# A routed expert layer: nine full expert tiles behind half of the dispatch, thirty behind all of it, and shared tiles among them

## The reference

```python
h = _layernorm(x, axis=-1) * (1 + ca) + sa
x = x + ga * _L0_attn_ref(h, ...)     # 1024 training steps of a small MLP, then q through it
h = _layernorm(x, axis=-1) * (1 + cb) + sb
x = x + gb * _L0_ffn_ref(h, ...)
```

```python
logits = jnp.einsum('btd,ed->bte', x, w_router)
probs = jax.nn.softmax(logits, axis=-1)
vals, idx = jax.lax.top_k(probs, TOP_K)                  # TOP_K = 2
hs = jax.nn.gelu(jnp.einsum('btd,fd->btf', x, Ws1) + bs1)
acc = jnp.einsum('btf,df->btd', hs, Ws2) + bs2
h = jax.nn.gelu(jnp.einsum('btd,efd->btef', x, W1) + b1)
y = jnp.einsum('btef,edf->bted', h, W2) + b2
return SCALE * (acc + jnp.einsum('bted,bte->btd', y, gates))
```

## Time and profile before

| | us |
|---|---|
| median of 3 runs | 688.48 (681.39 to 690.98) |
| profiled execution | 682.79 |
| its span, first to last instruction | 680.9 |
| PE, DVE, POOL, ACT busy | 594.7, 428.7, 350.4, 315.2 |
| 39 expert tiles, first to last product | 148.6 |

### The profile page before, as it was taken

How to read it: one execution, slowest core, us unless ns; L and a number is a source line. 1 busy time by engine, 2 the same in 40 slices (tenths; PEclk the granted TensorE clock), 3 DMA queues, 4 the chain that set the end, 5 groups by cost and what they waited for, 6 DMA issues and landing times. The chain is left out here.

```text
span 680.9 us, 14547 instructions
## 1 busy us (share of the span) xinstructions
PE 594.7 (87%) x4322; PEld 519.4 (76%) x4322; DVE 428.7 (63%) x1766; ACT 315.2 (46%) x996; POOL 350.4 (51%) x556
## 2 busy tenths in 40 slices
PE   1459999999999999999965898899399999999927
PEld 1339999999999999999843776677289989999912
DVE  2846888888888888888847767374044545445406
ACT  1455666666666666666513342353044444434300
POOL 1025666666666666666526386575615455454520
PEclk9999999999999999999978787889799999999969
DMA  9059900000000000000000011111737678787457
GB/s 213 6 230 414 410 32 1 1 0 0 0 0 0 0 0 0 0 0 1 2 0 1 4 49 37 40 45 38 221 88 215 217 212 239 210 230 227 145 183 210
DMA packets 42739, 66.76 MB, mean 98 GB/s; under 512 B 7394, under 2 KB 30692, under 8 KB 42692
## 3 DMA queue, kind: packets, MB, share of 16 engines
q1 hardware_dynamic: 31908, 52.74, 25.0%
q0 software_dynamic: 4544, 9.45, 3.8%
q10 hardware_dynamic: 6240, 4.00, 2.2%
HBM read 36.25 MB, written 29.92 MB: 97 GB/s over the span
## 5 line engine op out<-in xcount | busy, mean ns | idle before, releaser
L1770 POOL DMA_INDIRECT ys<-yo,dst x78 | 74.6, 957 | 87.7 <-DVE yo L1685 71.8
L1473 ACT ACTIVATE hid<-bank,slab 128x256 f32<-128x256 f32 x156 | 63.5, 474 | 87.9 <-PE bank L1364 79.5
L1762 POOL DMA_INDIRECT xs<-hrow,slot_i x64 | 68.9, 1077 | 35.1 <-issue 23.8
L1375 PEld LDWEIGHTS bank<-slab,hid 128*128 128x128 f32 x624 | 75.6, 192 | 2.0
L1364 PE MATMUL bank<-hg,slab 128*128 128x256 f32 x312 | 74.7, 382 | 1.7 <-issue 0.7
L1375 PE MATMUL bank<-slab,hid 128*128 128x128 f32 x624 | 75.8, 275 | 0.0
L1364 PEld LDWEIGHTS bank<-hg,slab 128*128 128x128 f32 x312 | 56.2, 190 | 9.5 <-issue 2.5
L1465 ACT ACTIVATE hs<-bank,sb 128x256 f32<-128x256 f32 x64 | 26.2, 474 | 62.7 <-PE bank L1330 42.0
L1346 PE MATMUL bank<-sw,hs 128*128 128x128 f32 x256 | 37.7, 304 | 9.9 <-ACT hs L1465 7.4
L1346 PEld LDWEIGHTS bank<-sw,hs 128*128 128x128 f32 x256 | 34.1, 212 | 16.1 <-ACT hs L1465 10.5
L1668 DVE SCALAR_TENSOR_TENSOR row<-xt,etab 128x2 f32<-128x2 f32 x39 | 8.6, 220 | 58.1 <-DMA ys<-yo,dst 48.5
(11 more groups left out here) (313 smaller groups left out, 1813.7 us busy)
## 6 DMA issues: line engine op xcount, KB each, us to landing
slab<-in_slabs_dram SPq DMA_DIRECT2D x39, 578.0 KB
xs<-fill SPq DMA_DIRECT2D x34, 528.0 KB
xt<-xs SPq DMA_DIRECT2D x39, 132.0 KB
xr<-in_L_attn_x_dram SPq DMA_DIRECT2D x8, 256.0 KB, 8.9
yg<-ys SPq DMA_DIRECT2D x4, 512.0 KB, 8.8
yg<-ys ACTq DMA_DIRECT2D x4, 512.0 KB, 9.7
ys<-yo,dst POOLq DMA_INDIRECT x78
xs<-hrow,slot_i POOLq DMA_INDIRECT x64
```

What stands on the lines that cost most here:

```text
L1375: mm = pe.matmul(bank[4 + j % 2][:, s * D:(s + 1) * D], hid[j % 2][:, n, s * P:(s + 1) * P], slab[j % RW][:, F + n * P:F + (n + 1) * P], s ...
L1473: nc.scalar.activation(hid[j % 2][:, n, :], e_half(j, n), ACT.Gelu_apprx_tanh, bias=slab[j % RW][:, 2 * F + n:2 * F + n + 1]).then_inc(e_x, 1)
L1762: pool.indirect_dma_start(out=xs[:, :], out_offset=bass.IndirectOffsetOnAxis(ap=slot_i[:, i, c:c + 1], axis=0), in_=hrow[:, c, :], in_offs ...
L1770: pool.indirect_dma_start(out=ys[:, :], out_offset=bass.IndirectOffsetOnAxis(ap=dst[r][:, s:s + 1], axis=0), in_=yo[r][:, s, :], in_offset ...
```

## The change

The layer and its tiles are the same. These parts of the order and of the work differ:

1. **Attention output.** DVE adds the result to x in all groups (`x1`); POOL adds the bias row in groups 0 and 1 only, and in the other six a product of PE with the whole group (L1318) brings the bias. The first hidden product goes ahead of the bias product.
2. **Normalising.** ACT normalises (`normalise`, four activations a group, to `xn`), PE turns that, and ACT applies the batch rows' scale and shift on the turned tile (`modulate`, four activations a group). DVE makes the rows to be dispatched with two operations on a whole group (`rows`). `spread` is written with scalar_tensor_tensor and has one root step of higher order and one of Newton's in place of three of Newton's.
3. **Routing** in four parts of two groups, as before in size; its steps start earlier beside the shared tiles. Two tables: `full_tiles` after part 1 names nine tiles that are full by then, as half the tokens fill at least nine whatever they choose; `other_tiles` after part 3 names the other thirty.
4. **Dispatch** counts on two semaphores, one for each half of the tokens. The nine full tiles need the first, the thirty the second. POOL sends the last part's DMAs between the scatters of the first four expert tiles.
5. **Shared tiles.** Nine run before the experts; four go between the first expert tiles (after each second) and three stand behind the last, in the same pipeline of jobs.
6. **The end.** A token's rows in `ys` are numbered by partition and then chunk, so that a group's load is one piece of 4 KB per partition; SP issues all eight loads.

```diff
-SG = 8
-NSG = CH // SG
-GSG = SG // GRP
-TSG = SG // SUB
+PARTS = ((0, 2), (2, 4), (4, 6), (6, 8))
+LONGEST = 8
+EARLY = 2
+N_FULL = -(-(B * S - E * (TS - 1)) // TS)
+EARLY_SH = 9
+JOBS = []
+for n in range(N_FULL):
+    JOBS.append(("expert", n))
+    if n % 2 and n // 2 < 4:
+        JOBS.append(("shared", EARLY_SH + n // 2))
+JOBS += [("expert", n) for n in range(N_FULL, N_TILES)]
+JOBS += [("shared", n) for n in range(EARLY_SH + 4, N_SH)]
...
-            ys_v = ys[0:2 * B * S, :].rearrange("(c p k) d -> p c (k d)", p=P, k=2)
+            ys_v = ys[0:2 * B * S, :].rearrange("(p c k) d -> p c (k d)", p=P, k=2)
...
-                sp.wait_ge(table_ready, 2)
-                for j in range(RW):
-                    weights(j)
-                sp.wait_ge(s_disp, 16 * 2 * CH)
-                for j in range(N_TILES):
-                    if j >= RW + 2:
-                        weights(j - 2)
-                weights(N_TILES - 2)
-                weights(N_TILES - 1)
+
+                sp.wait_ge(table_ready, 2)
+                for j in range(RW):
+                    weights(j)
+                sp.wait_ge(s_half[0], 16 * CH)
+                for j in range(N_FULL):
+                    rows(j)
+                    if j >= RW:
+                        weights(j)
+                sp.wait_ge(table_ready, 4)
+                weights(N_FULL)
+                weights(N_FULL + 1)
+                sp.wait_ge(s_half[1], 16 * CH)
+                for j in range(N_FULL, N_TILES):
+                    rows(j)
+                    if j >= N_FULL + 2:
+                        weights(j)
                 all_scattered(sp)
-                for g in range(0, NG, 2):
+                for g in range(NG):
                     load(sp, g)
...
+                    if g >= EARLY:
+                        pe.matmul(bank[2 + g % 2][:, :], ones[:, :], diag[:, :].unsqueeze(1).broadcast_to([P, GRP, D]),
+                                  start=True, stop=False, skip_group_check=True)
                     for j in range(GRP):
                         mm = pe.matmul(bank[2 + g % 2][:, j * P:(j + 1) * P], qa[g][:, j * P:(j + 1) * P], W2[:, :],
-                                       start=True, stop=True)
+                                       start=(g < EARLY), stop=True, skip_group_check=True)
```

PE's order, POOL's order and the numbering of a token's rows:

```diff
                 pe.matmul(bank[7][:, 0:D], wqT[:, :], W1[:, :], start=True, stop=True).then_inc(wz_ready, 1)
+                pe.wait_ge(wz_copied, 1)
+                hidden(0)
                 pe.wait_ge(d_ready, 1)
                 pe.matmul(bank[6][:, 0:D], ones[:, :], diag[:, :], start=True, stop=True).then_inc(b_ready, 1)
-                pe.wait_ge(wz_copied, 1)
-                hidden(0)
                 hidden(1)
+                result(0)
+                result(1)
                 hidden(2)
-                result(0)
                 hidden(3)
-                result(1)
                 hidden(4)
                 hidden(5)
                 result(2)
+                result(3)
                 hidden(6)
                 hidden(7)
-                result(3)
-                result(4)
                 turn(0)
                 turn(1)
                 route(0)
+                result(4)
+                places(0)
+                turn(2)
+                turn(3)
                 result(5)
+                up(0)
+                route(1)
                 result(6)
-                places(0)
                 result(7)
-                for k in range(1, NSG):
-                    t = (k - 1) * TSG
+                places(1)
+                turn(4)
+                turn(5)
+                down(0)
+                up(1)
+                route(2)
+                down(1)
+                up(2)
+                places(2)
+                turn(6)
+                turn(7)
+                down(2)
+                up(3)
+                route(3)
+                down(3)
+                up(4)
+                places(3)
+                down(4)
+                for t in range(5, EARLY_SH):
                     up(t)
-                    up(t + 1)
                     down(t)
+                pe.wait_ge(slot_ready, len(PARTS))
+                pe.wait_ge(x_ready, FT * EARLY_SH)
+                pe.wait_ge(post_ready, EARLY_SH)
+                feed_for(0)
+                feed_for(1)
                 e_up(0)
-                for j in range(N_TILES):
-                    if j + 2 < N_TILES:
-                        feed(j + 2)
-                    if j + 1 < N_TILES:
-                        e_up(j + 1)
-                    e_down(j)
+                for i in range(len(JOBS)):
+                    feed_for(i + 2)
+                    if i + 1 < len(JOBS):
+                        e_up(i + 1)
+                    e_down(i)
...
-                for g in range(4):
+                for g in range(EARLY):
                     add_bias(g)
-                for g in range(3):
-                    add_result(g)
-                for g in range(4, NG):
-                    add_bias(g)
-                for g in range(3, BY_POOL):
-                    add_result(g)
-                for k in range(NSG):
-                    dispatch(k)
-                for j in range(N_TILES):
+                for k in range(3):
+                    dispatch(k, *chunks(k))
+                c0, c1 = chunks(3)
+                for j in range((c1 - c0) // 2):
+                    scatter(j)
+                    dispatch(3, c0 + 2 * j, c0 + 2 * j + 2)
+                for j in range((c1 - c0) // 2, N_TILES):
                     scatter(j)
...
-        2 * (_np.arange(CH)[None, :] * P + _np.arange(P)[:, None]),
+        2 * (_np.arange(P)[:, None] * CH + _np.arange(CH)[None, :]),
```

DVE's list of calls:

```diff
-                times_gate(0)
-                times_gate(1)
+                def x1(g):
+                    times_gate(g)
+                    add_result(g)
+
+                x1(0)
                 statistics(0)
-                times_gate(2)
+                x1(1)
                 statistics(1)
                 spread(0)
-                normalise(0)
-                times_gate(3)
-                times_gate(4)
+                x1(2)
+                statistics(2)
+                x1(3)
+                statistics(3)
+                spread(1)
+                rows(0)
                 choose(0)
-                times_gate(5)
+                rows(1)
                 gates(0)
                 slots(0)
+                x1(4)
+                statistics(4)
+                x1(5)
+                statistics(5)
+                choose(1)
+                spread(2)
+                gates(1)
+                slots(1)
                 times_gate(6)
                 times_gate(7)
+                rows(2)
+                rows(3)
+                full_tiles()
+                post(0)
                 add_result(6)
+                statistics(6)
                 add_result(7)
-                for k in range(1, NSG):
-                    t = (k - 1) * TSG
-                    for g in range(k * GSG, (k + 1) * GSG):
-                        statistics(g)
-                    spread(k)
-                    normalise(k)
+                statistics(7)
+                choose(2)
+                spread(3)
+                post(1)
+                gates(2)
+                slots(2)
+                rows(4)
+                rows(5)
+                choose(3)
+                post(2)
+                gates(3)
+                slots(3)
+                rows(6)
+                rows(7)
+                other_tiles()
+                for t in range(3, EARLY_SH):
                     post(t)
-                    post(t + 1)
-                    choose(k)
-                    post(t + 2)
-                    gates(k)
-                    slots(k)
-                tables()
-                for t in range(N_SH - TSG, N_SH):
-                    post(t)
-                for j in range(2):
-                    e_high(j)
-                    meta(j)
-                for j in range(N_TILES):
-                    if j + 2 < N_TILES:
-                        e_high(j + 2)
-                        meta(j + 2)
-                    e_post(j)
+                prepare(0)
+                prepare(1)
+                for i in range(len(JOBS)):
+                    prepare(i + 2)
+                    e_post(i)
```

New functions of ACT (`normalise`, `modulate`) and of DVE (`rows`, the tables):

```diff
+                def normalise(g):
+                    k = part(g)
+                    act.wait_ge(r_ready, k + 1)
+                    if k >= 2:
+                        act.wait_ge(turned, PARTS[k - 1][0])
+                        act.wait_ge(scaled, PARTS[k - 1][0])
+                    for j in range(GRP):
+                        c = g * GRP + j
+                        n = nc.scalar.activation(normal(g, j), xr[:, c, :], ACT.Identity,
+                                                 bias=nmr[:, c:c + 1], scale=rstd[:, c:c + 1])
+                    n.then_inc(xn_ready, 1)
+
+                def modulate(g):
```

(37 more changed lines are left out.)

428 lines of the change are left out of this document (239 added, 189 removed).

## The result

The changed kernel takes **705.77 us** (701.22 to 710.71), the kernel before 685.62 in the runs of the same comparison: a ratio of 1.0291, 95% interval [1.0165, 1.0417]. The forecast of 668 and its range up to 695 are missed, on the slow side. The profiled execution took 710.08, its span is 708.0.

What follows compares the result with a forecast made beforehand. PE was taken to bound the expert tiles, with idle time to win around them. First expert tile at 469.9 plus 179.0 of jobs, 17 of drain and 1.9 around gave 668 us; range 650 to 695.

Steps and rivals of the forecast that it cites:

- Up to the first dispatch: Attention output and first routing part: DVE becomes the bound, and POOL starts dispatching at 386 us, not 388.7.
- The late signals: Ahead of the first expert tile: delayed signals near the slab loads cost 12 us, moving its start from 457.9 to 469.9.
- the rival on the reload: Final reload of ys slows to the slab loads' 219 GB/s, taking 19 us in place of 12: 674; chance 0.08.
- Rival 2: Dispatch without a pause: some 8 PE handoffs to DVE late, 43 us in place of 12: 699; chance 0.12.
- theory A: Formed after the result: over some ten POOL indirect DMAs in a row at 1.26 us slow other engines' issue and signals.
- No cost: Expert jobs: POOL's last 16 dispatch DMAs among four scatters fall 6.8 us behind, within the four tiles' lead.
- rival 3: Expert jobs: interleaving starves them, POOL's lag of 6.8 us adding to the wait for tile 9: 675; chance 0.12.
- Part 4, the drain: After PE's last product: reload mostly beside three shared tiles, end 17 us later in place of 33.4, gain 16.4.
- the prediction's 20 us: Final reload: its time by the skill page's 207 GB/s for large power-of-two pitches; the prediction took 351 GB/s instead.
- rival 1: Ahead of the first expert tile: no late signals in the chain, 12 us less: 656; chance 0.16.
- the chain without late signals: DVE's routing chain, then PE's shared tiles: first expert tile could start at 457.9, against 498.9 before.

Runs made afterwards that it cites:

- the DMAs 1.67 us apart: The changed kernel with a POOL memset of 128x512 behind each dispatch DMA and no wait for landings: 664.79 us, ratio to before 0.9588.
- the kernel with late loads: The changed kernel with the first five slab loads issued only once the first 32 dispatch DMAs have landed: 708.89 us, ratio to before 1.0231.

## Why the prediction was wrong

**Up to the first dispatch: right.** Forecast 386, measured 387.3. The second spread took 2.8 us (372.39 to 375.18; 3.05 forecast, 7.57 for the first before), choose 3.1 as forecast; no operation of DVE was stretched to 1.2 us. Dispatch of 32 took 40.4 us (45.2 forecast, with a DMA of 3.37 us in each 16 that didn't come).

**The failed step: "The late signals".** It took 12 us, from the 17.2 of the chain of before, and put the first expert product at 469.9; it came at 498.0, 28.1 late. With the DMAs 1.67 us apart it comes at 461.4, with no wait on "remote" before it, so the term of 12 measured 36.6 against that kernel. Three readings in that step were wrong.
- It read the price in a schedule where POOL paused after each 16 DMAs, and carried it over to one where it doesn't. The step says itself that the waits lie in the later part of each batch; a wait that grows with the length of a batch grows when two batches are joined.
- It said that no row tells the cause, but placed the price where the slab loads stand and read their 13.49 us as their own time. They were an effect, as the kernel with late loads shows, and so was the bound of 219 GB/s in the rival on the reload: 4.19 MB came in 11.4 us, 367 GB/s.
- It counted late signals only. The issue of instructions on PE, DVE and SP is slowed too, so work that waits for nobody takes longer: 21 us for sixteen products that took 1.95 before.

Rival 2, the slower one, had the mechanism ("if signals are late for as long as POOL goes on") and gave 699; its 0.12 was too low. The evidence held against it, one post in the middle of a batch that ended with PE's own row, is what theory A expects there. It priced 43 us in place of 12, near the 36.6 measured, but by eight late signals of 5.4 us each, and left out the jobs. The trace has fewer and longer ones, three on DVE with 29.9 us (below the 40 that the prediction named as this rival's sign), and the slowed issue beside them; that 699 came close is in part luck.

**Second failed step: "No cost" for the interleaving in part 3.** The jobs took 191.1 us in place of 179.0: PE idle in 8.3, the rest at a lower clock (0.96 over the stretch). The loss sits between 512 and 542, with PE busy in 21.7 of 30 us at a granted clock of 0.81. POOL's queue was counted against its own deadline, which it kept; what it did to the others was not. With spaced DMAs the jobs take 184.0, and of these 3.9 are the wait for tile 9, which rival 3 named and put at 6.8.

**Part 4, the drain: right in mechanism, 1.9 short.** 18.9 us in place of 17. The sums start 0.1 us after PE's last job at full clock, so no part of the reload shows. DVE waits for PE in each group, 1.72 us apart where I had DVE's 1.44:

```profile
699.61 0.69 DVE L1910 TENSOR_TENSOR ysum<-bank,gate 128x512 f32<-128x512 f32 x1 [0.30 <-PE bank L1495]
...
701.32 0.69 DVE L1910 TENSOR_TENSOR ysum<-bank,gate 128x512 f32<-128x512 f32 x1 [0.30 <-PE bank L1495]
```

The reload in the new numbering was the faster of the two. The Trainium skill, "DMA: Bandwidth & Descriptors", section "Latency and other measured facts", has pitches of a large power of two go slower. Its figures begin at 512 KiB, and they are of copies between two DRAM tensors, where it calls 214 GB/s the full rate; so its 207 at 512 KiB didn't bear on a reload with a pitch of 32 KB, which ran at 367 GB/s, and the prediction's 20 us misread it. No run here has a pitch that the page measured.

**The sum.** 28.1 for the first expert product, 12.1 for the jobs and 1.9 for the drain are the 42.1 us between 665.9 and the span of 708.0. The rest of the working stands: with the DMAs spaced, the first expert product is at 461.4 where the chain without late signals gave 457.9, and the whole takes 664.8, between rival 1's 656 and the forecast. Part of the 3.5 us between is PE's clock. PE waits 4.7 us for DVE, goes on at 440.90 at half the full clock (0.50 granted up to 445.60, 1.2 GHz), and then does the sixteen down products of a tile in 3.78 us in place of 2.05. The shared tiles after that take 4.34 us each, where the prediction had 4.9 for a tile alone.

## What to carry to other kernels

A pause in one engine's queue can be what keeps others going: before a wait is taken away or two batches are joined, look at what the others do at the end of the longest unbroken run that the trace has. Instructions in step, at equal distances, with "issue" before them and nothing to wait for, are a sign of their own, and are read in the timeline, not in a sum of waits. And where work is thinned by idle time on purpose (0.4 us more between two DMAs), the gain can be larger than that of the change that it repairs: 41 us here, where the repaired change beats the kernel before by 28.

## What the runs showed of the hardware

- POOL's indirect DMAs of 128 rows, one per 1.26 us, slow the issue on PE, DVE and SP, over long stretches to one instruction per 0.7 or 1.4 us, and ACT waited up to 14.8 us for a signal. The first late signal seems to be that of the products from 393.86 on, six DMAs in; DVE's reader of them, for whose start the trace names no releaser:

```profile
403.82 0.23 DVE L1721 TENSOR_TENSOR pos<-bank,base 128x64 f32<-128x64 f32 x1 [5.97 <-issue]
```

- It clears some 5 us after the last of them is issued (427.67 and 432.5). POOL itself is hardly disturbed: of the 31 steps between the first 32 DMAs 28 are 1.26 or 1.27 us and three 1.6 to 1.7. Up to the first expert product none of the late signals is left at 1.67 us, and at 1.35 the effect is whole.
- What resource they share stays open. The Trainium skill, "NOTIFIC — the notification-queue block", section "7.1 Overflow: three behaviours, one of which stalls the engine", states that this block's internal pipeline always holds its producers back rather than lose a record. That could look like this; but all executions shown here were recorded, so no run tells whether the recording takes part. That rows or bytes decide rather than DMAs is open too.
- A stretch of 9.7 us without work cost PE 2.4 us more in the sums behind it, at a mean granted clock of 0.85.
